# Cross-attention on one core: row tiles weighed two at a time, and the output projection of 14 batches in products of fp16 parts

## The chip, the cores and the metric

One core of a Trainium2 chip runs the whole program. The metric is the device time of one execution in microseconds (us), as the median over several runs of the same kernel. TensorE does the matrix products (the profile shows its products as PE and its weight loads as PEld), VectorE is DVE, ScalarE is ACT, GpSimd is POOL, SyncE is SP. SP computes nothing here: it issues nearly all DMA transfers, and its row in the trace is the time that it spends on issuing them.

## The reference, cut to what matters

For each of B = 16 batches there are 100 query rows (`x`) and 1444 context rows (`ctx`), all 128 wide; there are H = 16 heads of width 64.

```python
q = (x @ Wq + bq).reshape(b, 100, 16, 64)
k = (ctx @ Wk + bk).reshape(b, 1444, 16, 64)
v = (ctx @ Wv + bv).reshape(b, 1444, 16, 64)
attn = softmax(einsum('bqhd,bkhd->bhqk', q, k) / 8)
out = einsum('bhqk,bkhd->bqhd', attn, v).reshape(b, 100, 1024) @ Wo + bo
z = x + out
result = (z - mean(z)) * rsqrt(var(z) + 1e-5) * gamma + beta
```

## The kernel before, in words

**The algebra.** The kernel never forms keys or values. For each head it folds the key weights into the query (`a_sb`, 128x128 a head) and the value weights into the output weights (`m_sb`, 128x128 a head, in 32-bit floats). For a batch it projects the queries (`project_queries`, L390, and from batch 3 on `project_queries_16`, L396, of fp16 parts), scores them against the context itself, weighs the context itself with the softmax, and projects the weighed context out with `m_sb` (`project_out`, L403).

**Row tiles.** The 16 x 100 = 1600 (head, query) rows of a batch are cut in tiles of 128. A batch fills 12.5 tiles, so two batches share 25: tiles 0 to 11 of the even batch, tile 12 (the mixed tile) half of each, tiles 13 to 24 of the odd batch. There are N = 200 tiles in all.

**Precision.** Every large operand is split in two fp16 parts, hi and lo. The scores of a tile are three products (hi x hi, hi x lo, lo x hi) over three stretches of 482, 482 and 480 keys, nine instructions (L537). The weighing of a tile (`weigh`, L540) takes the softmax transposed, with the keys in 12 blocks of 128: for 11 blocks `pt_hi` against `c_hi` and `c_lo` (22 products of 128 columns, L551), then 12 products with `pt_lo` (L556). The weights are the context block, the moving operand is the softmax tile. All 34 add up in 128 columns of one PSUM bank (`O_BANK`), in the mixed tile twice 34 products of 64 columns.

**One tile through the engines.** PE scores tile n into one of two sets of three banks (L537). DVE takes the row maximum (L757). ACT takes the exponential and the row sum (L871); DVE takes the reciprocal (L763, L765); ACT writes the hi part `p_hi` (L879), and DVE the lo part `p_lo` (L772). SP transposes both by DMA (`transpose_hi`, L331, issue at L336; `transpose_lo`, L338, issue at L344) into `pt_hi` and `pt_lo`, rings of PTS = 3 tiles; each transpose waits until the tile that had its place is weighed. PE weighs tile n in its iteration n + LAG, LAG = 4. ACT copies the result out of `O_BANK` into `o_t`, scaled back (`take_result`, L889), and only then may PE start the next weighing.

**The loop of PE** (L609) is, for each n: scores of tile n, weighing of tile n - 4, and a job. The order is written out by hand, and every engine works through its own list in that order. `window(n)` (L89) gives the batch w whose tiles are scored and the place r in it, 0 to 12. The jobs are set by r: the queries of batch w + 1 in four groups of four heads at r = 1 to 4 (moved by DVE at L700, split by POOL in `split_queries`, L958); the output projection of batch w - 1 in four groups of four heads at r = 6 to 9 (`FIN_AT`, L582 to L595), a 128x128 32-bit product a head with the 100 `o_t` columns as weights; the spreading of a maximum at r = 10 (L455). At r = 9 DVE adds the residual and takes mean and variance (`take_rows`, L781), and POOL finishes the rows (`inverse_deviation`, L991, and `scale_rows`, L998). DVE also takes the maximum of the context of batch w + 2 at r = 6 to 8, ACT makes `c_hi` at r = 4, 6 and 7 (L853), POOL makes `c_lo` (L975). SP loads context at r = 1 to 3 and stores a result at r = 2. After the last tile come four weighings with parts of the last output projection between them (L623 to L630), and the rows of the last batch.

**PSUM.** Banks 0 to 5 are the scores, 6 is `O_BANK`, 7 is `JOB_BANK`.

## Time and profile before

| | |
|---|---|
| Median of 3 runs | 902.93 us (902.35 to 903.62) |
| The profiled execution: its own time | 902.63 us |
| Its span, first to last instruction | 900.7 us |
| Mean granted TensorE clock | 0.989 |
| Busy: PE, PEld, DVE, ACT, POOL | 880.5, 678.1, 812.7, 752.2, 335.9 us |
| Moved by DMA | 181.17 MB, mean 201 GB/s |

The profile shows one execution. Products are pipelined, so one of them is shown longer than the distance at which they follow each other; the distance is read from how long a run of them takes in the chain of waits. "DMA share" is the time that packets took as a share of the 16 engines' time; packets overlap, so it can be above 1. "SPq" is SP's queue.

### The profile page before, as it was taken

The page shows a single profiled execution, that of the slowest core. Times are in us where ns is not written, and L with a number is a line of the kernel's source. Part 1 is how long each engine was busy: PE and PEld are TensorE (multiplying, and loading weights), DVE is VectorE, ACT ScalarE, POOL GpSimd, SP SyncE. Part 2 cuts the span into 40 slices and gives each one's busy share as a digit, 9 for nine tenths or more (in the row PEclk, how much of TensorE's full clock was granted, in tenths as well). Part 3 has the DMA queues.
Part 4 walks back from the last instruction along what each step waited for, and adds up shares of the span by engine and source line. Part 5 has one row for each costly group of instructions (what it writes and reads, how often), then busy time and mean ns, then how long its engine had stood idle before and what let it go on. Part 6 is the DMA issues. An engine that isn't in the chain of part 4 may idle for free.

```text
span 900.7 us, 25456 instructions
## 1 busy us (share of the span) xinstructions
PE 880.5 (98%) x10366; PEld 678.1 (75%) x10366; DVE 812.7 (90%) x1042; ACT 752.2 (84%) x1081; POOL 335.9 (37%) x385
## 2 busy tenths in 40 slices
PE   8799989999999999999999999999999999999997
PEld 7476877777777777777777777777777777777776
DVE  4899879999999999989999999999999999998983
ACT  3687878888888888888889888888888889888983
POOL 3042596534415253342424434152442525144011
PEclk8899999999999999999999999999999999999999
DMA  8598998999999999999999999999999999999996
GB/s 235 130 181 176 187 192 165 211 209 201 222 206 207 215 200 215 199 211 221 206 216 210 209 211 218 214 205 212 206 224 199 207 221 196 205 204 204 204 172 121
DMA packets 683065, 181.17 MB, mean 201 GB/s; under 512 B 654596, under 2 KB 682052, under 8 KB 682948
## 3 DMA queue, kind: packets, MB, share of 16 engines
q1 hardware_dynamic: 681332, 178.48, 105.1%
q8 instruction: 82, 1.34, 0.7%
q10 hardware_dynamic: 1344, 0.53, 0.2%
q0 software_dynamic: 272, 0.53, 0.2%
q14 instruction: 35, 0.29, 0.1%
HBM read 15.35 MB, written 0.82 MB: 18 GB/s over the span
## 4 chain that ended last, share of the span: by engine, by line
PE 89%; DVE 4%; POOL 3%; ACT 2%; issue 1%; DMA 1%; POOLq 0%; SPq 0%; DVEq 0%; ACTq 0%
PE ps L537 38%; PE ps L551 26%; PE ps L556 14%; PE ps L405 6%; PE ps L399 3%; DVE nmax L757 1%; DVE p_lo L772 1%; PE ps L392 1%; ACT p L871 1%; POOL early_sb L1017 1%; PE ps L458 1%; POOL c_lo L986 1%; DMA o_t<-in_L_xattn_Wq_dram 1%; POOL x_sb L1048 1%; POOL c_scaled L1015 0%
## 5 line engine op out<-in xcount | busy, mean ns | idle before, releaser
L772 DVE SCALAR_TENSOR_TENSOR p_lo<-p,rinv,p_hi 128x1444 f16<-128x1444 f32 x200 | 347.5, 1738 | 6.5 <-ACT p_hi L879 6.1
L879 ACT ACTIVATE p_hi<-p,rinv 128x1444 f16<-128x1444 f32 x200 | 299.8, 1499 | 49.3 <-DVE rinv L765 33.9
L757 DVE TENSOR_REDUCE nmax<-ps 128x1 f32<-128x1446 f32 x200 | 329.8, 1649 | 7.4 <-PE ps L537 7.4
L871 ACT ACTIVATE p<-ps,nmax 128x1446 f32<-128x1446 f32 x200 | 292.0, 1460 | 13.2 <-DVE nmax L757 12.9
L551 PE MATMUL ps<-pt_hi,c_hi 128*128 128x128 f16 (+1 forms) x2288 | 269.2, 217 | 0.7 <-ACT o_t L894 0.7
L551 PE MATMUL ps<-pt_hi,c_lo 128*128 128x128 f16 (+1 forms) x2288 | 269.1, 217 | 0.0
L551 PEld LDWEIGHTS ps<-pt_hi,c_hi 128*128 128x128 f16 x2288 | 217.5, 98 | 24.8 <-issue 3.4
L551 PEld LDWEIGHTS ps<-pt_hi,c_lo 128*128 128x128 f16 x2288 | 217.3, 98 | 20.3 <-issue 0.3
L537 PE MATMUL ps<-ct_hi,g_hi 128*128 128x482 f16 (+3 forms) x624 | 156.8, 370 | 1.6 <-DVE ps L727 0.9
L556 PE MATMUL ps<-pt_lo,c_hi 128*128 128x128 f16 (+1 forms) x2288 | 157.0, 217 | 0.0
L537 PE MATMUL ps<-ct_hi,g_lo 128*128 128x482 f16 (+3 forms) x624 | 156.2, 368 | 0.0
L537 PE MATMUL ps<-ct_lo,g_hi 128*128 128x482 f16 (+3 forms) x624 | 155.8, 367 | 0.0
L963 POOL CAST g_hi<-g_raw 128x400 f16<-128x400 f32 x60 | 31.0, 517 | 304.3 <-DVE g_raw L700 304.3
L556 PEld LDWEIGHTS ps<-pt_lo,c_hi 128*128 128x128 f16 x2288 | 132.2, 98 | 0.0
L894 ACT ACTIVATE o_t<-ps,unscale 128x128 f32<-128x128 f32 (+1 forms) x208 | 73.9, 359 | 65.2 <-PE ps L556 64.3
L986 POOL TENSOR_TENSOR c_lo<-c_scaled,c_hi 128x512 f16<-128x512 f32 x45 | 87.0, 1932 | 77.3 <-ACT c_hi L853 73.3
L537 PEld LDWEIGHTS ps<-ct_hi,g_lo 128*128 128x128 f16 (+1 forms) x624 | 59.0, 99 | 64.9 <-issue 1.5
L537 PEld LDWEIGHTS ps<-ct_lo,g_hi 128*128 128x128 f16 (+1 forms) x624 | 59.0, 99 | 64.9 <-issue 1.5
L537 PEld LDWEIGHTS ps<-ct_hi,g_hi 128*128 128x128 f16 (+1 forms) x624 | 53.6, 100 | 25.8 <-issue 2.6
L886 ACT ACTIVATE p_lo<-p,rinv 128x72 f16<-128x72 f32 x200 | 69.9, 349 | 0.0
L405 PE MATMUL ps<-m_sb,o_t 128*100 128x128 f32 x512 | 68.7, 277 | 0.2 <-ACT o_t L894 0.2
L763 DVE TENSOR_SCALAR rsum<-psums 128x1 f32<-128x1 f32 x200 | 30.6, 153 | 35.3 <-ACT p L871 26.4
(108 smaller groups left out, 728.0 us busy)
## 6 DMA issues: line engine op xcount, KB each, us to landing
c_raw<-in_ctx_dram SPq DMA_DIRECT2D x32, 256.0 KB
pt_hi<-p_hi SPq DMA_TRANSPOSE x200, 3.5
pt_lo<-p_lo SPq DMA_TRANSPOSE x200, 3.9
c_raw<-in_ctx_dram SPq DMA_DIRECT2D x16, 192.0 KB
c_raw<-in_ctx_dram SPq DMA_DIRECT2D x48, 18.0 KB
out_dram<-late_sb SPq DMA_DIRECT2D x16, 50.0 KB
x_sb<-in_x_dram SPq DMA_DIRECT2D x1, 600.0 KB
o_t<-in_L_xattn_Wq_dram SPq DMA_DIRECT2D x2, 256.0 KB, 4.3
```

What stands on the lines that cost most here:

```text
L405: mm = pe.matmul(bank[0:QL, 0:P], o_t[:, par, h * QL:(h + 1) * QL], m_sb[:, h, :], start=(h == 0), stop=(h == H - 1), skip_group_check=True)
L537: mm = pe.matmul(ps[at:at + rows, bank + k, 0:e - a], g, ct, start=(part == 0), stop=(part == 2))
L551: pe.matmul(out_t, c[:, b % 2, t, :], pt_hi[:, n % PTS, t, at:at + rows], start=(t == 0 and c is c_hi), stop=False)
L556: mm = pe.matmul(out_t, c, pt_lo[:, n % PTS, t, at:at + rows], start=False, stop=(t == KT - 1))
L757: dve.tensor_reduce(nmax[:, n % RING:n % RING + 1], ps[:, bank:bank + 3, 0:KEYW], AX.XY, ALU.max, negate=True).then_inc(s_nm, 1)
L772: dve.scalar_tensor_tensor(out=p_lo[:, n % LOS, 0:KL], in0=p32[:, n % P32S, 0:KL], scalar=rinv[:, i:i + 1], in1=p_hi[:, par, 0:KL], op0=AL ...
L871: act.activation(p32[:, n % P32S, :].rearrange("p (k w) -> p k w", w=KEYW), ps[:, bank:bank + 3, 0:KEYW], ACT.Exp, bias=nmax[:, i:i + 1], ...
L879: act.activation(p_hi[:, par, 0:KL], p32[:, n % P32S, 0:KL], ACT.Copy, scale=rinv[:, i:i + 1]).then_inc(s_hi, 1)
L886: act.activation(p_lo[:, n % LOS, KL:KL + 2 * KTAIL].rearrange("p (i k) -> p i k", i=2), tail, ACT.Copy, scale=rinv[:, i:i + 1]).then_inc( ...
L894: act.activation(o_t[:, b % 2, row:row + rows], ps[:, O_BANK, at:at + rows], ACT.Copy, scale=unscale[:, b % UNSCALES:b % UNSCALES + 1]).th ...
L963: pool.tensor_copy(g_hi[:, par, cols], query_group(g)).then_inc(s_part, 1)
L986: pool.tensor_tensor(c_lo[:, par, tiles, :].rearrange("p t d -> p (t d)"), c_scaled[:, :], c_hi[:, par, tiles, :].rearrange("p t d -> p (t ...
```

## The change

Row tiles are joined in units: tiles (0,1), (2,3) to (10,11), the mixed tile alone, (13,14) to (23,24), 13 units in a pair of batches. `pt_hi` and `pt_lo` now hold three units. A unit of two is weighed by the same 34 weights, each with a moving operand of 2 x 128 columns, into 256 columns of the bank. In the iteration that is 4 after the unit's first tile PE does the products of the first nine hi blocks (18 products), in the next one the other two hi blocks and the lo blocks (4 + 12 products). The mixed tile is weighed as before. ACT takes a unit's result in one instruction of 256 columns, in the second of these iterations. After the last tile the last unit is weighed in two parts between parts of the last output projection.

For batches 1 to 14 the output projection takes three fp16 products a head (hi x hi, lo x hi, hi x lo). `m16`, the parts of `m_sb`, is made once: maxima by DVE at n = 17 to 20, the spread and the scale at n = 22, hi by ACT at n = 23 to 26, lo by POOL in window 2. `o16`, the parts of `o_t`, is made by POOL for each of the 14 batches, group by group, in front of `split_queries` of the same group, and the last group after the fourth. The scaling back moves from ACT's copy to DVE's residual addition, with a factor that POOL makes (`output_scale`). The rows of the last batch are finished by DVE instead of POOL. `m16` and `o16` lie in the memory of `a_sb` and `xT`.

Core of the diff (semaphores, small tiles and blank lines left out):

```diff
-    assert HALF == P // 2
+    assert HALF == P // 2 and WHOLE % 2 == 0
     IN_PAIR = 2 * WHOLE + 1
     MIXED = WHOLE
-    SEGS = WHOLE + 1
+    UNITS = WHOLE + 1
+    RESULTS = WHOLE // 2 + 1
...
+    FIRST_TILES = 9
...
+    def unit(n):
         pair, i = divmod(n, IN_PAIR)
-        return 2 * SEGS * pair + i + (1 if i > MIXED else 0)
+        u, place = divmod(i, 2) if i < MIXED else (MIXED // 2, 0) if i == MIXED else divmod(i + 1, 2)
+        return UNITS * pair + u, place
+    def tiles_of(u):
+        pair, j = divmod(u, UNITS)
+        first = IN_PAIR * pair + 2 * j - (1 if j > MIXED // 2 else 0)
+        return (first,) if j == MIXED // 2 else (first, first + 1)
+    def results_of(u):
+        tiles = tiles_of(u)
+        if len(tiles) == 1:
+            return segments(tiles[0])
+        b, row, rows, at = segments(tiles[0])[0]
+        return ((b, row, 2 * P, 0),)
...
+    def in_parts(b):
+        return 0 < b < B - 1
...
-        pt_hi = sb("pt_hi", [P, PTS, KT - 1, P], F16)
-        pt_lo = sb("pt_lo", [P, PTS, KT, P], F16)
+        pt_hi = sb("pt_hi", [P, PTS, 2, KT - 1, P], F16)
+        pt_lo = sb("pt_lo", [P, PTS, 2, KT, P], F16)
...
+        m16 = a_sb[:, :, :].rearrange("p h e -> p (h e)").bitcast(F16).rearrange("p (h i e) -> p h i e", i=2, e=P)
+        o16 = xT[:, :, :].rearrange("p b q -> p (b q)").bitcast(F16).rearrange("p (i r) -> p i r", i=2)
...
+        MPARTS_AT = 17
+        MTOP_AT = IN_PAIR // 2 + TOP_AT
+        M16_AT = MTOP_AT + 1
...
             def transpose_hi(n):
                 par = n % 2
                 sp.wait_ge(s_hi, n + 1)
-                if n >= PTS:
-                    sp.wait_ge(s_pv, segments_before(n - PTS + 1))
-                sp.dma_start_transpose(pt_hi[:, n % PTS, :, :], p_hi[:, par, 0:(KT - 1) * P]).then_inc(s_th[par], 16)
+                u, place = unit(n)
+                if u >= PTS:
+                    sp.wait_ge(s_pv, results_before(u - PTS + 1))
+                sp.dma_start_transpose(pt_hi[:, u % PTS, place, :, :], p_hi[:, par, 0:(KT - 1) * P]).then_inc(s_th[par], 16)
...
+            def project_out_16(bank, heads):
+                for h in heads:
+                    rows = slice(QL * h, QL * (h + 1))
+                    for i, j in ((0, 0), (1, 0), (0, 1)):
+                        mm = pe.matmul(bank[0:QL, 0:D], o16[:, i, rows], m16[:, h, j, :], start=(h == 0 and i == j),
+                                       stop=(h == H - 1 and j == 1))
                 return mm
...
-            def weigh(n):
-                par = n % 2
-                for i, (b, row, rows, at) in enumerate(segments(n)):
-                    out_t = ps[:, O_BANK, at:at + rows]
-                    if n > 0:
-                        pe.wait_ge(s_ot, segments_before(n))
+            def weigh_hi(u, tiles, first):
+                if first and u > 0:
+                    pe.wait_ge(s_ot, results_before(u))
+                for n in tiles_of(u):
+                    pe.wait_ge(s_th[n % 2], halves(n))
+                for b, row, rows, at in results_of(u):
+                    if first and tiles_of(u)[0] == first_tile(b):
+                        pe.wait_ge(s_chl, b + 1)
+                    weigh_part(u, b, rows, at, [(c, pt_hi, t) for t in tiles for c in (c_hi, c_lo)], first, False)
+            def weigh_lo(u):
+                for n in tiles_of(u):
+                    pe.wait_ge(s_tl[n % LOS], turns(n))
+                for b, row, rows, at in results_of(u):
+                    weigh_part(u, b, rows, at, [(c_hi, pt_lo, t) for t in range(KT - 1)] + [(c_tail, pt_lo, KT - 1)],
+                               False, True).then_inc(s_pv, 1)
+            def weigh_mixed(u):
+                n, = tiles_of(u)
+                pe.wait_ge(s_ot, results_before(u))
+                for b, row, rows, at in results_of(u):
                     if n == first_tile(b):
                         pe.wait_ge(s_chl, b + 1)
-                    pe.wait_ge(s_th[par], halves(n))
-                    for t in range(KT - 1):
-                        for c in (c_hi, c_lo):
-                            pe.matmul(out_t, c[:, b % 2, t, :], pt_hi[:, n % PTS, t, at:at + rows],
-                                      start=(t == 0 and c is c_hi), stop=False)
+                    pe.wait_ge(s_th[n % 2], halves(n))
+                    weigh_part(u, b, rows, at, [(c, pt_hi, t) for t in range(KT - 1) for c in (c_hi, c_lo)], True, False)
                     pe.wait_ge(s_tl[n % LOS], turns(n))
-                    for t in range(KT):
-                        c = c_hi[:, b % 2, t, :] if t < KT - 1 else c_tail[:, b % 2, :]
-                        mm = pe.matmul(out_t, c, pt_lo[:, n % PTS, t, at:at + rows], start=False, stop=(t == KT - 1))
-                    mm.then_inc(s_pv, 1)
+                    weigh_part(u, b, rows, at, [(c_hi, pt_lo, t) for t in range(KT - 1)] + [(c_tail, pt_lo, KT - 1)],
+                               False, True).then_inc(s_pv, 1)
+            def weigh_part(u, b, rows, at, products, first, last):
+                out_t = ps[:, O_BANK, at:at + rows]
+                for i, (c, pt, t) in enumerate(products):
+                    weights = c_tail[:, b % 2, :] if c is c_tail else c[:, b % 2, t, :]
+                    moving = pt[:, u % PTS, 0, t, at:at + rows] if rows < P else pt[:, u % PTS, :, t, :]
+                    mm = pe.matmul(out_t if rows < P else split(out_t, 2, P), weights, moving, start=(first and i == 0),
+                                   stop=(last and i == len(products) - 1))
+                return mm
+            def weigh(n):
+                if 0 <= n - LAG < N:
+                    u, place = unit(n - LAG)
+                    if len(tiles_of(u)) == 1:
+                        weigh_mixed(u)
+                    elif place == 0:
+                        weigh_hi(u, range(FIRST_TILES), True)
+                if 0 <= n - LAG - 1 < N:
+                    u, place = unit(n - LAG - 1)
+                    if len(tiles_of(u)) == 2 and place == 0:
+                        weigh_hi(u, range(FIRST_TILES, KT - 1), False)
+                        weigh_lo(u)
...
-                        pe.wait_ge(s_ot, SEGS * w)
-                    mm = project_out(bank, (w - 1) % 2, range(HG * g, HG * (g + 1)))
+                        if w == 1:
+                            pe.wait_ge(s_ot, RESULTS * w)
+                        else:
+                            pe.wait_ge(s_ml, NG)
+                    if in_parts(w - 1):
+                        pe.wait_ge(s_os, NG * (w - 2) + g + 1)
+                        mm = project_out_16(bank, range(HG * g, HG * (g + 1)))
+                    else:
+                        mm = project_out(bank, (w - 1) % 2, range(HG * g, HG * (g + 1)))
...
+                    if n == MTOP_AT:
+                        pe.wait_ge(s_mc, 1)
+                        pe.matmul(bank[:, P:2 * P], spread(m_max[:, :]), ident[:, :], start=True, stop=True).then_inc(s_mt, 1)
...
+            last = unit(N - 1)[0]
+            pe.wait_ge(s_z, B - 1)
+            done = project_last(0, last - 1)
+            weigh_hi(last, range(KT - 1), True)
+            done = project_last(done, last)
+            weigh_lo(last)
+            pe.wait_ge(s_ot, 2 * RESULTS * (B // 2))
+            project_out(ps[:, JOB_BANK, :], (B - 1) % 2, range(done, H)).then_inc(s_fin, 1)
...
+        def finish_rows(eng, b):
+            par = b % 2
+            eng.wait_ge(s_rd, b + 1)
+            eng.tensor_scalar(zn[:, par, :], z[:, par, :], mv[:, par, 0:1], rstd[:, par:par + 1], ALU.subtract,
+                              ALU.mult).then_inc(s_zn, 1)
+            eng.wait_ge(s_zn, b + 1)
+            eng.tensor_tensor(zg[:, par, :], zn[:, par, :], rows_b[0:QL, 1, :], ALU.mult).then_inc(s_zg, 1)
+            eng.wait_ge(s_zg, b + 1)
+            if b > 1:
+                eng.wait_ge(s_out[par], 16 * (b // 2))
+            eng.tensor_tensor(y[:, par, :], zg[:, par, :], rows_b[0:QL, 2, :], ALU.add).then_inc(s_y, 1)
...
+                if in_parts(b):
+                    dve.wait_ge(s_fu, b)
+                    dve.scalar_tensor_tensor(out=z[:, par, :], in0=ps[0:QL, JOB_BANK, 0:D], scalar=fin_un[0:QL, par:par + 1],
+                                             in1=x_sb[:, b, :], op0=ALU.mult, op1=ALU.add).then_inc(s_z, 1)
+                else:
+                    dve.tensor_tensor(z[:, par, :], ps[0:QL, JOB_BANK, 0:D], x_sb[:, b, :], ALU.add).then_inc(s_z, 1)
...
             take_rows(B - 1)
+            finish_rows(dve, B - 1)
...
-            def take_result(n):
-                for i, (b, row, rows, at) in enumerate(segments(n)):
-                    act.wait_ge(s_pv, segments_before(n) + len(segments(n)))
+            def take_result(u):
+                for i, (b, row, rows, at) in enumerate(results_of(u)):
+                    act.wait_ge(s_pv, results_before(u) + len(results_of(u)))
                     if row == 0 and b > 1:
                         act.wait_ge(s_fin, b - 1)
                     act.activation(o_t[:, b % 2, row:row + rows], ps[:, O_BANK, at:at + rows], ACT.Copy,
-                                   scale=unscale[:, b % UNSCALES:b % UNSCALES + 1]).then_inc(s_ot, 1)
+                                   scale=O_PART if in_parts(b) else unscale[:, b % UNSCALES:b % UNSCALES + 1]).then_inc(s_ot, 1)
+            def take_results(n):
+                if n - LAG < N and len(tiles_of(unit(n - LAG)[0])) == 1:
+                    take_result(unit(n - LAG)[0])
+                if n > LAG and unit(n - LAG - 1)[1] == 0 and len(tiles_of(unit(n - LAG - 1)[0])) == 2:
+                    take_result(unit(n - LAG - 1)[0])
...
+                if M16_AT <= n < M16_AT + NG:
+                    g = n - M16_AT
+                    act.wait_ge(s_ms, 1)
+                    if g == 0:
+                        act.wait_ge(s_16, NG)
+                    act.activation(m16[:, HG * g:HG * g + HG, 0, :], m_sb[:, HG * g:HG * g + HG, :], ACT.Copy,
+                                   scale=m_scale[:, :]).then_inc(s_mh, 1)
...
+            def split_results(b, g):
+                pool.wait_ge(s_ot, results_taken(b, HG * QL * (g + 1)))
+                if g == 0 and b > 1:
+                    pool.wait_ge(s_fin, b)
+                cols = query_columns(g)
+                pool.tensor_copy(o16[:, 0, cols], o_t[:, b % 2, cols]).then_inc(s_oh, 1)
+                pool.wait_ge(s_oh, NG * (b - 1) + g + 1)
+                pool.tensor_tensor(o16[:, 1, cols], o_t[:, b % 2, cols], o16[:, 0, cols], ALU.subtract).then_inc(s_os, 1)
+            def output_scale(b):
+                pool.wait_ge(s_mu, 1)
+                if b > 2:
+                    pool.wait_ge(s_z, b - 1)
+                pool.tensor_scalar(fin_un[:, b % 2:b % 2 + 1], unscale[:, b % UNSCALES:b % UNSCALES + 1], m_un[:, :], 1.0 / O_PART,
+                                   ALU.mult, ALU.mult).then_inc(s_fu, 1)
+            def leave_m_lo(g):
+                heads, at = slice(HG * g, HG * g + HG), c_scaled[:, :].rearrange("p (n w) -> p n w", w=P)
+                pool.wait_ge(s_mh, g + 1)
+                if g:
+                    pool.wait_ge(s_ml, g)
+                pool.tensor_scalar(at, m_sb[:, heads, :], m_scale[:, :], 1.0, ALU.mult, ALU.mult).then_inc(s_mw, 1)
+                pool.wait_ge(s_mw, g + 1)
+                pool.tensor_tensor(m16[:, heads, 1, :], at, m16[:, heads, 0, :], ALU.subtract).then_inc(s_ml, 1)
...
+                        if w == 2:
+                            leave_m_lo(g)
+                        if g < NG - 1 and in_parts(w - 1):
+                            split_results(w - 1, g)
                         split_queries(b, g)
+                    if w == 2:
+                        pool.wait_ge(s_ml, NG)
+                if in_parts(w - 1):
+                    if b == B:
+                        for g in range(NG - 1):
+                            split_results(w - 1, g)
+                    split_results(w - 1, NG - 1)
+                    output_scale(w - 1)
+                if b < B:
...
-                    scale_rows(w - 1)
+                    finish_rows(pool, w - 1)
             inverse_deviation(B - 1)
-            scale_rows(B - 1)
```

## Rows read from the trace of the kernel before

**Rows 1.** Stretches: a pair of batches, then a plain, a query and a projection tile.

```profile
core 0: us, PE busy (x) PEld busy (x) DVE busy (x) ACT busy (x) POOL busy (x), PEclk, DMA share, GB/s
406.30:512.17 105.87, 105.87 (x1285) 81.46 (x1286) 100.24 (x127) 92.38 (x133) 39.71 (x46) 1.00 1.15 214
457.52:461.26 3.74, 3.74 (x45) 2.77 (x43) 3.71 (x5) 3.52 (x5) 0.00 (x0) 1.00 1.21 256
473.55:477.83 4.28, 4.28 (x57) 3.31 (x55) 4.25 (x7) 3.67 (x5) 1.62 (x3) 1.00 0.93 222
490.49:495.13 4.64, 4.64 (x52) 3.67 (x51) 4.61 (x6) 4.16 (x7) 0.67 (x1) 1.00 1.12 175
```

**Rows 2.** Chain of waits, start us, us, what: PE's kinds of work.

```profile
92.50 0.92 PE ps L392 x8
...
418.28 0.54 PE ps L399 x12
...
431.19 1.84 PE ps L537 x9
433.03 1.23 PE ps L551 x22
434.26 0.67 PE ps L556 x12
434.93 0.91 PE ps L405 x8
```

**Rows 3.** Groups of instructions, shapes apart: count, busy us, mean ns, idle before.

```profile
L551 PEld LDWEIGHTS ps<-pt_hi,c_hi 128*128 128x128 f16 x2288 | 217.5, 98 | 24.8 <-issue 3.4 <-ACT o_t L894 1.3
L537 PEld LDWEIGHTS ps<-ct_hi,g_lo 128*64 128x64 f16 x48 | 2.7, 110 | 2.2
L405 PEld LDWEIGHTS ps<-m_sb,o_t 128*100 128x100 f32 x512 | 58.3, 167 | 0.4 <-ACT o_t L894 0.4
L963 POOL CAST g_hi<-g_raw 128x400 f16<-128x400 f32 x60 | 31.0, 517 | 304.3 <-DVE g_raw L700 304.3
L965 POOL TENSOR_TENSOR g_lo<-g_raw,g_hi 128x400 f16<-128x400 f32 x60 | 56.8, 947 | 4.9
L853 ACT ACTIVATE c_hi<-c_raw,alpha 128x512 f16<-128x512 f32 x48 | 33.7, 707 | 0.3 <-DVE alpha L694 0.3
```

**Rows 4.** Order of time on ACT, over one plain tile: start us, us, instruction.

```profile
843.23 1.50 ACT L879 ACTIVATE p_hi<-p,rinv 128x1444 f16<-128x1444 f32 x1 [0.17 <-DVE rinv L765]
844.74 0.37 ACT L894 ACTIVATE o_t<-ps,unscale 128x128 f32<-128x128 f32 x1
845.00 1.46 ACT L871 ACTIVATE p<-ps,nmax 128x1446 f32<-128x1446 f32 x1
...
846.97 1.50 ACT L879 ACTIVATE p_hi<-p,rinv 128x1444 f16<-128x1444 f32 x1 [0.18 <-DVE rinv L765]
```

**Rows 5.** SP's queue: issues of tile 91, then of tile 109 (hi parts).

```profile
434.91 1.42 SPq L336 DMA_TRANSPOSE pt_hi<-p_hi  x1
...
509.55 1.53 SPq L336 DMA_TRANSPOSE pt_hi<-p_hi  x1
```

**Rows 6.** The tile pt_hi: from issue to landing.

```profile
DMA to landing us min/median/max: 3.1/3.5/6.0
```

**Rows 7.** Chain of waits again: the weighings that started in iterations 94 and 112.

```profile
437.68 1.23 PE ps L551 x22
...
514.13 1.33 PE ps L551 x22
```

**Rows 8.** Order of time: the rows of the last batch.

```profile
894.95 0.29 DVE L787 TENSOR_TENSOR late_sb<-ps,x_sb 100x128 f32<-100x128 f32 x1 [7.36 <-PE ps L405]
...
896.87 0.81 POOL L1001 TENSOR_SCALAR late_sb<-late_sb,mv,rstd 100x128 f32<-100x128 f32 x1
897.76 0.46 POOL L1004 TENSOR_TENSOR late_sb<-late_sb,rows_b 100x128 f32<-100x128 f32 x1
898.29 0.45 POOL L1008 TENSOR_TENSOR late_sb<-late_sb,rows_b 100x128 f32<-100x128 f32 x1
```

97 lines of the change are left out of this document (65 added, 32 removed).

## The prediction

> **What bounds the kernel now.** I read the stretches first. In a pair of batches PE works 105.87 of 105.87 us at a granted clock of 1.00; DVE works 100.24, ACT 92.38, POOL 39.71 [rows 1]. So PE has no gap at all in the steady part, and each us taken from its list is a us of the run until the next engine is met. That is DVE, 5.6 us a pair below. The chain of waits says the same: it stays on PE, from line to line without a wait, from about 135 us to 874 us, and [rows 2] is what it passes. Nine score products take 1.84 us. The 34 weighing products take 1.23 + 0.67 = 1.90 us. That is a plain tile, 3.74 us. Four heads of queries add 0.54 us, four heads of output projection 0.91 us (4.28 and 4.64 us [rows 1]).
>
> The distance between products shows what a product costs. 34 products of 128 columns in 1.90 us are 55.8 ns each; 128 columns at 2.4 GHz, the clock granted there, are 53.3 ns. The query products of 100 columns stand 0.54 / 12 = 45 ns apart, against 41.7 of streaming, the scores 204 ns apart against 200.8 for 482 columns [rows 2]. So streaming sets the distance, with 2.5 to 3.6 ns on top of each product. The weight load of 98 ns [rows 3] is no limit: it is longer than the distance of 55.8 and still delays nothing.
>
> **Weighing by two.** A unit of two tiles had 68 products of 128 columns, 2 x 1.90 = 3.79 us. It gets 34 of 256 columns. The columns are the same, half of the fixed parts go. With 106.7 ns of streaming and 2.5 to 3.6 ns on top, the unit takes 3.71 to 3.75 us and 44 to 82 ns are saved. I take 3.0 ns: 65 ns, and for 96 units **6.2 us** (4.2 to 7.9). Halving the number of weight loads gives nothing more, since they were covered.
>
> **The output projection.** 16 heads in four groups of 0.905 us (4.645 - 3.74 [rows 1]) are 3.62 us a batch. After: 48 fp16 products with 128 moving columns. The nearest row is the weighing's, 55.8 ns, so 2.68 us. Saved: 0.94 us a batch, in 14 batches **13.2 us**. The doubt is in the weights: `o16` is 100 columns wide, and no row has an fp16 load of 100 columns. The rows around it: 98 ns for 128 fp16 columns, but 110 ns for 64, so narrower loads are not quicker; 167 ns for 100 columns of 32 bits, which stand at 0.91 / 8 = 113 ns [rows 2, 3]. There the reported load is longer than the distance too, so part of it is always latency. Where a load does bind is the 32-bit query projection, 128 weight columns against 100 moving ones: 0.92 / 8 = 115 ns [rows 2], more than the 83 ns of its two passes of streaming; that is 0.9 ns a column of 32 bits. Half the bytes make 0.45 ns a column, some 45 ns for 100, covered by 55.8. The dear end is the 113 ns at which the 32-bit load of the same shape passes: 48 of them are 5.4 us, 1.8 us more than now, +25 us in 14 batches. The cheap end is 45 ns, the query product's distance: 2.14 us, 20.7 us saved. I take 55.8.
>
> The Trainium skill (TensorE: Matmul & The Clock Gate, Weight-path perf modes) says that the fast weight load applies only with 128 weights of a type other than FP32, and (LDWEIGHTS) that a plain load takes its columns over 1.2 GHz. By that an `o16` load is an estimated 83 ns, the projection 4.0 us a batch and the change here a loss of 5 us instead of a gain of 13. The row of 110 ns for 64 columns against 98 ns for 128 agrees that the narrow load is the slower kind; how long it holds PE no row shows.
>
> **What is added beside PE.** POOL splits the results: for each group a cast and a subtraction as for the queries, 0.52 + 0.95 = 1.46 us [rows 3], so 5.9 us a batch, 12 us a pair on 39.71 of 106. POOL's queue is in order, so what stands behind matters: `split_queries`, `context_lo`, the rows. Groups 0 to 2 wait for results that were taken in an earlier window; the last waits for the batch's last result, at r = 3 or 4, and is done at about r = 5, while PE asks for it at r = 9. `context_lo` waits for `c_hi` at r = 4, 6 and 7 anyway, and POOL was idle 304 us in front of its casts alone [rows 3]. I take nothing; without this cover it would cost its 5.9 us a batch. DVE's added instruction replaces one of its kind.
>
> Once only: `m16` costs DVE four maxima, ACT 4 x 0.71 us (the `c_hi` copy, of this shape) [rows 3] at n = 23 to 26, where tiles are shortest, POOL four groups in window 2, PE one product (0.3 us). ACT falls behind by up to 2 us there. I take 0.3 for PE and 0.7 us for late transposes after it; POOL's part (some 22 us from n = 26) ends just before PE asks for it at n = 31.
>
> **ACT's copy.** 208 copies become 112, wider. From a unit's first to its second iteration ACT saves one. A plain tile's loop through ACT and DVE is hi part to hi part 3.74 us, in which the copy takes 0.27 (844.73 to 845.00) [rows 4]. Without a copy it is 3.47, with a wide one, growing with the columns, about 3.85: 3.66 on average. PE's plain tile will be 3.71. This loop stays below PE, narrowly.
>
> **The wait that the change moves.** A unit's first products need the hi transposes of both tiles. The second tile's has to be there three iterations after its scores, not four. In tile 109, a second tile, the issue was at 509.55 us, landing 3.5 us later at 513.05, and iteration 112's weighing started at 514.13: 1.1 us to spare [rows 5 to 7]. In tile 91, also a second tile, it was issued at 434.91, landed at 438.41, and iteration 94's weighing began at 437.68: 0.7 us too late. I went through 92 of the 96 second tiles this way: four would be late, by 0.1 to 0.9 us, and eleven more have less than 1 us to spare, most of them behind the context loads (r = 3 to 5) or at r = 9 to 12. Two things shift that: PE's three tiles get shorter by 0.2 to 0.6 us, which takes; and the ring of three units frees the transposes from waiting for the weighing just before, which held back those of query and projection tiles by 0.5 to 0.9 us, and gives. I take **1.5 us** of stalls over the run (0 to 12). What waits behind PE then is only PE's own list.
>
> **The end.** DVE finishes the last rows instead of POOL: 0.81 + 0.46 + 0.45 us become three DVE instructions of about 0.29 [rows 8]: 0.85 us less. The last unit's result comes in one piece, which leaves three heads to project behind it where two stood: 0.25 us more. Net **0.6**.
>
> **Sum.** 900.7 - 6.2 - 13.2 - 0.6 + 0.3 + 0.7 + 1.5 = 883.2 us of span. The profiled execution took 902.63, so 1.9 us lie outside the span, and it stood 0.3 us below the median: 883.2 + 1.9 + 0.3 = 885.4, said as **885 us**. A pair of batches would take 105.87 - 12 x 0.065 - 8 x 0.235 = 103.2 us, above DVE's 100.2.
>
> **The rivals.**
> *Late transposes.* The odd hi parts keep missing the shorter deadline. For: SP issues nearly without a pause, and tile 91. Against: the margin of tile 109, and the freed ring. If two second tiles a window come 0.4 us late, 16 windows give 12.8 us in place of 1.5: 896 us.
> *The loop of ACT and DVE.* DVE's busy time is 97% of the new 103.2, and it works 4.25 of 4.28 us in a query tile [rows 1]. If waits between the engines hold a pair at 104.5, eight pairs give back 10 us: 895 us. Against: it needs losses that today's gapless PE doesn't show.
> *Loads of `o16` in the open (slower).* If a 100-column fp16 load holds PE for as long a column as the 32-bit one (0.9 ns), a product takes 90 ns, a batch 4.3 us, and 14 batches lose 10 us instead of gaining 13.2: 885.4 + 23 = 908 us. It decides from the distance of products: the other parts bring some 4 us, so above 3.62 + 4 / 14 = 3.9 us a batch, 81 ns a product, the change loses. For: the 110 ns of the narrow load. Against: half the bytes.
> *No gain from pairs.* If 256 columns in two strides cost 8 ns on top, weighing is where it was: 891 us.
>
> **How the numbers follow.** Forecast 0.62, late transposes 0.13, the loop 0.08, loads 0.08, no gain from pairs 0.09. The forecast's own range is 881 to 889. Against 902.93, 0.2% is 1.8 us, about what a measurement can tell from no change. All cases but the loads, and the far end of late transposes, are faster: 0.90; the same 0.04; slower 0.06. The range reaches down to 880 (2.5 ns on top and no stalls) and up to 897, which takes in the late transposes and leaves the loads out.
>
> **What would show it.** A pair of batches of 103.2 us; weighing products 109.7 ns apart and the unit at 3.73 us; four heads of fp16 projection in 0.67 us; PE without gaps in front of `weigh_hi`. Wrong if PE stands before a unit's first product on a transpose, if the twelve products of a group take over 0.9 us, or if PE's idle time grows to more than 3 us between 140 and 870 us.

## The result and the profile after

| | before | after |
|---|---|---|
| Median | 903.27 us (902.35 to 904.58, 4 runs) | 890.23 us (888.62 to 891.75, 4 runs) |
| Ratio | | 0.9849, 95% interval 0.9827 to 0.9870 |
| Profiled execution: own time, span | 902.63, 900.7 us | 888.62, 886.8 us |
| A pair of batches (tiles 75 to 99) | 105.87 us | 102.85 us |

The change makes the kernel 13.0 us faster. The forecast was 885 us, 5.2 us below what was measured. Of the executions of the experiments below one, of the run e11, took 1117.92 us at a mean granted clock of 0.749; no comparison uses it, and the other five of e11 have a median of 889.47 us. First the page's busy line of the kernel after, then two of its stretches, one of them a pair of batches without a stall, to set beside [rows 1]; the columns are those of the header.

```profile
PE 860.3 (97%) x7328; PEld 618.4 (70%) x7328; DVE 832.9 (94%) x1053; ACT 732.0 (83%) x989; POOL 483.2 (54%) x516
```

```profile
core 0: us, PE busy (x) PEld busy (x) DVE busy (x) ACT busy (x) POOL busy (x), PEclk, DMA share, GB/s
353.78:456.63 102.85, 102.85 (x908) 73.87 (x906) 101.05 (x127) 89.50 (x121) 60.59 (x64) 1.00 1.10 218
...
456.00:560.00 104.00, 102.87 (x907) 73.71 (x905) 101.42 (x124) 89.26 (x120) 60.00 (x64) 1.00 1.10 212
```

In the first stretch PE has no gap and DVE is 1.8 us below it. In the second PE idles 1.13 us. DVE is busier over the run than before (832.9 us against 812.7), although the change gives it little new to do (four maxima of 0.68 us and the last rows). The products, in the chain of waits (start us, us, what), against [rows 2]:

```profile
227.86 2.13 PE ps L642 x18
229.98 0.67 PE ps L458 x12
...
290.27 1.75 PE ps L642 x16
292.02 0.67 PE ps L458 x12
294.53 1.97 PE ps L642 x18
```

A unit's 16 + 18 products take 1.75 + 1.97 = 3.72 us, 109.4 ns a product; 18 products take 2.13 where they begin behind a stall. Four heads of the fp16 projection take 0.67 us, 56 ns a product, against 0.91 us. The costly groups of the kernel after (count, busy us, mean ns, idle before):

```profile
L921 DVE SCALAR_TENSOR_TENSOR p_lo<-p,rinv,p_hi 128x1444 f16<-128x1444 f32 x200 | 367.9, 1840 | 2.4 <-ACT p_hi L1038 2.0
...
L1147 POOL CAST xT<-o_t 128x400 f16<-128x400 f32 x56 | 88.9, 1588 | 13.1 <-ACT o_t L1053 13.1
L1149 POOL TENSOR_TENSOR xT<-o_t,xT 128x400 f16<-128x400 f32 x56 | 53.0, 947 | 4.6
...
L458 PEld LDWEIGHTS ps<-a_sb,xT 128*100 128x100 f16 x672 | 44.3, 125 | 2.3 <-issue 1.7
```

`p_lo` (L921, before L772 with a mean of 1738 ns) has grown by 102 ns, 20.4 us over 200 tiles: as much as DVE's whole 20 us. The cast of the results (L1147, into `o16`, which lies in `xT`) takes 1588 ns where the cast of the same shape took 517 [rows 3]. These two numbers are one thing. In order of time, DVE and POOL of the kernel after:

```profile
207.12 1.66 DVE L906 TENSOR_REDUCE nmax<-ps 128x1 f32<-128x1446 f32 x1
207.26 0.52 POOL L1137 CAST g_hi<-g_raw 128x400 f16<-128x400 f32 x1 [9.61 <-DVE g_raw L831]
207.86 0.95 POOL L1139 TENSOR_TENSOR g_lo<-g_raw,g_hi 128x400 f16<-128x400 f32 x1
208.69 1.71 DVE L921 SCALAR_TENSOR_TENSOR p_lo<-p,rinv,p_hi 128x1444 f16<-128x1444 f32 x1
208.75 2.02 POOL L1147 CAST xT<-o_t 128x400 f16<-128x400 f32 x1
210.86 0.95 POOL L1149 TENSOR_TENSOR xT<-o_t,xT 128x400 f16<-128x400 f32 x1
...
212.35 0.94 POOL L1139 TENSOR_TENSOR g_lo<-g_raw,g_hi 128x400 f16<-128x400 f32 x1
212.81 1.99 DVE L921 SCALAR_TENSOR_TENSOR p_lo<-p,rinv,p_hi 128x1444 f16<-128x1444 f32 x1
213.24 1.95 POOL L1147 CAST xT<-o_t 128x400 f16<-128x400 f32 x1
```

At 208.75 POOL's cast starts just behind `p_lo` and ends 2.02 us later, 0.37 us after `p_lo`: the cast waits for `p_lo`. At 212.81 `p_lo` starts while POOL is in a subtraction and takes 1.99 us in place of 1.71: `p_lo` waits for POOL. Sorted by what POOL was doing, the 67 `p_lo` with POOL idle average 1.72 us, the 12 that met mostly L1149 2.15, the 15 that met mostly L1139 2.02. The row maximum (L906), which reads PSUM, is 1.65 us beside any of them. What decides is how much of POOL's subtraction is left when `p_lo` starts: with 0.12 us left `p_lo` takes 1.71, with 0.48 left 1.99, with 0.57 left 2.08, with 0.64 left 2.15, so that what is added is 0.2 us less than what was left. The Trainium skill (SBUF — State Buffer, SBUF: two separate sides) states this: VectorE with two SBUF inputs and a GpSimd instruction that reads SBUF share a port pair by an exclusive lock, and the later one is blocked for the whole instruction of the earlier. The trace agrees for POOL's 128-row casts and subtractions, down to which of DVE's instructions is touched (`p_lo` has two inputs in SBUF). It does not fit POOL's scaling of 100 rows (L774): 14 `p_lo` start with 0.40 to 0.46 us of it left and take 1.71.

Where PE then stood. I measured the distance from tile to tile: the six pairs from tile 25 to 174 take 107.75, 103.36, 102.86, 104.15, 103.92 and 103.04 us. Six pairs without a stall would be 617.2, so 7.9 us are lost, 4.9 of them in the first. From 200 to 860 us PE waits only for transposes (us, times, the longest):

```profile
PE ps L642 <- DMA pt_hi<-p_hi: 3.3, 5, 1.1
```

Two of these waits, of 0.90 and 1.13 us, are of this kind (SP's queue, then the chain, then ACT in order of time, of the kernel after):

```profile
218.04 2.79 SPq L393 DMA_TRANSPOSE pt_hi<-p_hi  x1
220.89 0.58 SPq L348 DMA_DIRECT2D c_raw<-in_ctx_dram  x1
221.53 1.30 SPq L352 DMA_DIRECT2D c_raw<-in_ctx_dram  x3
222.94 1.30 SPq L402 DMA_TRANSPOSE pt_lo<-p_lo  x1
224.35 1.41 SPq L393 DMA_TRANSPOSE pt_hi<-p_hi  x1
```

```profile
223.65 0.70 ACT p_hi L1038
224.35 3.38 DMA pt_hi<-p_hi
227.72 0.14 issue
227.86 2.13 PE ps L642 x18
```

```profile
219.52 1.50 ACT L1038 ACTIVATE p_hi<-p,rinv 128x1444 f16<-128x1444 f32 x1 [0.46 <-DVE rinv L914]
```

The transpose of a second tile (41) stands behind a slow one, a context load and the three tail loads of r = 3; it is issued at 224.35, lands at 227.72, and PE, which had stood since 226.96, starts. The chain names ACT's `p_hi` of 223.65 as the releaser, and that is misleading: it is the `p_hi` of the next tile. That of tile 41 is the one of 219.52 and was over at 221.02, so the transpose stood 3.3 us in SP's queue with its input ready. The wait of 0.89 us (PE at 596.74) is of another kind: there the transpose stood 1.1 us in the queue and took 5.5 us to land, against a median of 3.5. The first pair has another stall, in order of time:

```profile
171.18 2.10 POOL L1163 TENSOR_SCALAR c_scaled<-m_sb,m_scale 128x512 f32<-128x512 f32 x1
...
173.37 1.16 POOL L1165 TENSOR_TENSOR a_sb<-c_scaled,a_sb 128x512 f16<-128x512 f32 x1
...
174.62 0.84 PE L458 MATMUL ps<-a_sb,xT 128*100 128x128 f16 x12 [1.44 <-issue]
```

PE waits 1.44 us for POOL's last lo part of m, and starts 0.1 us after it ended.

### The profile page after: what moved, and what is told of

The parts are those of the page before. It is cut to its first block, busy times and chain, and to the rows that moved or that the text cites. A ratio compares the mean times of both kernels' runs of the same rounds, so it can differ in the third digit from the quotient of the medians.

```text
span 886.8 us, 19588 instructions
## 1 busy us (share of the span) xinstructions
PE 860.3 (97%) x7328; PEld 618.4 (70%) x7328; DVE 832.9 (94%) x1053; ACT 732.0 (83%) x989; POOL 483.2 (54%) x516
## 4 chain that ended last, share of the span: by engine, by line
DVE 43%; PE 38%; issue 8%; ACT 5%; DMA 5%; SPq 2%; ACTq 0%; DVEq 0%; POOLq 0%; POOL 0%
DVE p_lo L921 20%; PE ps L642 17%; DVE nmax L906 16%; PE ps L603 16%; DMA pt_hi<-p_hi 4%; ACT p L1030 2%; PE ps L458 2%; ACT p_hi L1038 2%; DVE rsum L912 2%; PE ps L450 1%; DVE rinv L914 1%; DVE c_max L808 1%; PE ps L465 1%; DMA bq_pairs<-in_L_xattn_bq_dram 1%; SPq L402 1%
## 5 line engine op out<-in xcount | busy, mean ns | idle before, releaser
L921 DVE SCALAR_TENSOR_TENSOR p_lo<-p,rinv,p_hi 128x1444 f16<-128x1444 f32 x200 | 367.9, 1840 | 2.4 <-ACT p_hi L1038 2.0
L906 DVE TENSOR_REDUCE nmax<-ps 128x1 f32<-128x1446 f32 x200 | 330.0, 1650 | 6.0 <-PE ps L603 6.0
L642 PE MATMUL ps<-pt_hi,c_hi 128*128 128x256 f16 (+1 forms) x1232 | 253.6, 261 | 5.4 <-DMA pt_hi<-p_hi 3.8
L642 PE MATMUL ps<-pt_hi,c_lo 128*128 128x256 f16 (+1 forms) x1232 | 253.4, 261 | 0.0
L642 PEld LDWEIGHTS ps<-pt_hi,c_hi 128*128 128x128 f16 x1232 | 114.4, 98 | 43.0 <-issue 10.4
L642 PE MATMUL ps<-pt_lo,c_hi 128*128 128x256 f16 (+1 forms) x1232 | 138.7, 261 | 0.0
L642 PEld LDWEIGHTS ps<-pt_hi,c_lo 128*128 128x128 f16 x1232 | 113.8, 98 | 29.5 <-issue 0.5
L642 PEld LDWEIGHTS ps<-pt_lo,c_hi 128*128 128x128 f16 x1232 | 109.6, 98 | 11.9
L1186 POOL TENSOR_TENSOR c_lo<-c_scaled,c_hi 128x512 f16<-128x512 f32 x45 | 98.3, 2184 | 24.7 <-ACT c_hi L1012 22.1
L1147 POOL CAST xT<-o_t 128x400 f16<-128x400 f32 x56 | 88.9, 1588 | 13.1 <-ACT o_t L1053 13.1
L1139 POOL TENSOR_TENSOR g_lo<-g_raw,g_hi 128x400 f16<-128x400 f32 x60 | 58.0, 967 | 4.8
```

What stands on the lines that cost most here:

```text
L642: mm = pe.matmul(out_t if rows < P else split(out_t, 2, P), weights, moving, start=(first and i == 0), stop=(last and i == len(products) - 1))
L906: dve.tensor_reduce(nmax[:, n % RING:n % RING + 1], ps[:, bank:bank + 3, 0:KEYW], AX.XY, ALU.max, negate=True).then_inc(s_nm, 1)
L921: dve.scalar_tensor_tensor(out=p_lo[:, n % LOS, 0:KL], in0=p32[:, n % P32S, 0:KL], scalar=rinv[:, i:i + 1], in1=p_hi[:, par, 0:KL], op0=AL ...
L1139: pool.tensor_tensor(g_lo[:, par, cols], query_group(g), g_hi[:, par, cols], ALU.subtract).then_inc(s_gs, 1)
L1147: pool.tensor_copy(o16[:, 0, cols], o_t[:, b % 2, cols]).then_inc(s_oh, 1)
L1186: pool.tensor_tensor(c_lo[:, par, tiles, :].rearrange("p t d -> p (t d)"), c_scaled[:, :], c_hi[:, par, tiles, :].rearrange("p t d -> p (t ...
```

## The experiments

The theory: PE's list got shorter by about what was worked out, and the loss is stalls of PE, from transposes that came late because DVE and ACT were held up through the port shared with POOL. The rival: the second tile's shorter deadline alone. "Lost" below is the time of tiles 25 to 174 over six pairs without a stall (102.86 us each, 104.48 without the fp16 projection; e9, e11 and e12 have 0.8 us of one 32-bit projection in it). It and `p_lo` come from one profiled execution each, the medians from 4 to 12 executions; for e2 there is no pair without a wait to compare with. The two do not always agree: the profiled execution was the fastest of the four in the changed kernel (888.62) and the slowest of the four in e7 (894.25) and e10 (887.57), and in the profiled executions tile 25 starts anywhere from 141.9 to 145.9 us.

| run | median us | ratio (95%) | lost | `p_lo` ns |
|---|---|---|---|---|
| the changed kernel | 890.23 | 0.9849 (0.9827 to 0.9870) | 7.9 | 1840 |
| e1 pairs alone | 895.83 | 0.9905 (0.9887 to 0.9923) | 0.5 | 1751 |
| e2 parts alone | 898.21 | 0.9931 (0.9915 to 0.9948) | - | 1834 |
| e3 no splits | 885.12 | 0.9789 (0.9770 to 0.9809) | 4.3 | 1761 |
| e4 no lo part of m | 887.33 | 0.9807 (0.9784 to 0.9829) | 5.2 | 1830 |
| e5 before, with splits | 903.82 | 0.9995 (0.9983 to 1.0006) | 0 | 1775 |
| e6 LAG 5 | 891.76 | 0.9868 (0.9853 to 0.9884) | 8.0 | 1829 |
| e7 casts twice | 891.21 | 0.9864 (0.9845 to 0.9882) | 11.5 | 1790 |
| e8 LAG 5, no splits | 887.37 | 0.9814 (0.9799 to 0.9829) | 2.4 | 1749 |
| e9 m later | 889.80 | 0.9840 (0.9821 to 0.9859) | 7.2 | 1834 |
| e10 loads spread | 885.49 | 0.9793 (0.9774 to 0.9812) | 4.8 | 1831 |
| e11 all three | 889.78 | 0.9840 (0.9824 to 0.9856) | 6.9 | 1823 |
| e12 e9 with e10 | 886.41 | 0.9813 (0.9789 to 0.9836) | 5.6 | 1825 |

The ratios are to the kernel before in the same comparison.

**e1, the pairs alone.**

```diff
     def in_parts(b):
-        return 0 < b < B - 1
+        return False
```
(and the instructions that make `m16` and its scale are left out)

> The units of two tiles alone, the output projection in 32 bits as before, nothing added on POOL. In the changed kernel a unit's products stand 109.2 ns apart, so 96 units save 8 us, and the last rows on DVE about 0.6. Theory of the port (POOL's added casts and subtractions stretch DVE's p_lo, DVE falls behind, the hi transposes come late and PE stands): without the added POOL work there are no stalls, 894.5 us, p_lo 1.74 us as before. Rival, the shorter deadline of the second tile (three iterations in place of four): it is here as it was, so the stalls stay and 3 to 7 us of the gain are lost: 897 to 901 us.

895.83 us, 0.9905. Pairs of batches of 104.48 to 104.53 us but for one of 104.93. Between 200 and 860 us PE waited on nothing but this:

```profile
PE ps L642 <- DMA pt_hi<-p_hi: 0.4, 1, 0.4
```

With PE's list at 104.48 us a pair, 1.6 us longer than in the changed kernel, the deadline alone costs 0.4 us. The rival falls in this form; e3 has the deadline together with the short list.

**e2, the parts alone.**

```diff
     def tiles_of(u):
-        pair, j = divmod(u, UNITS)
...
+        return (u,)
```
(a unit is one tile; weighing, copies and the weighings at the end as in the kernel before, the last rows stay on DVE)

> The fp16 output projection alone, tiles weighed one at a time, each with four iterations for its transposes. PE's list gets 14 x 0.94 = 13.2 us shorter and POOL's added work is all there. Theory of the port: p_lo rises to some 1.82 us, some 5 us are lost around the splitting of m and little after: 894 to 896 us. Rival, the shorter deadline: it is not here, so there are no stalls and the 13.2 us come in full, with 0.6 from the end: 889.5 us.

898.21 us, a gain of 0.69% where by the prediction's working the list got 13.2 us shorter: 7 us lost, without any shorter deadline, and 2 us more than the theory said. Windows 2 and 3 take 108.3 us, the later pairs 104.35 to 105.2, and PE waits for `o_t`, ACT's copy, which it never did before:

```profile
PE ps L632 <- ACT o_t L1036: 1.8, 6, 0.3
```

The two halves add up: 0.9905 x 0.9931 = 0.9837, within the interval of both together.

**e3, POOL's splits left out.**

```diff
-                pool.tensor_copy(o16[:, 0, cols], o_t[:, b % 2, cols]).then_inc(s_oh, 1)
...
-                pool.tensor_tensor(o16[:, 1, cols], o_t[:, b % 2, cols], o16[:, 0, cols], ALU.subtract).then_inc(s_os, 1)
+                pool.tensor_copy(o16[0:1, 0, cols.start:cols.start + 1], o_t[0:1, b % 2, cols.start:cols.start + 1]).then_inc(s_os, 1)
```
(`o16` is a tile of its own that stays zero but for single elements: the kernel leaves the 14 projections out of its result, while PE does the same products)

> The changed kernel with POOL's splitting of the results left out (o16 is a tile of its own and stays zero but for single elements, so the projection adds nothing; PE's products are the same). Left: the splitting of m in window 2. Theory of the port: p_lo falls from 1.84 to about 1.77 us, DVE gains some 13 us of slack, the stalls of the steady part go (2 to 4 us) and window 2 loses less: 885 to 887 us. Rival, the shorter deadline: within 1 us of the changed kernel, 890.

885.12 us, as the theory had it, with `p_lo` back at 1761 ns:

```profile
L921 DVE SCALAR_TENSOR_TENSOR p_lo<-p,rinv,p_hi 128x1444 f16<-128x1444 f32 x200 | 352.1, 1761 | 2.5 <-ACT p_hi L1038 2.2
```

But 2.2 of the 3.0 us of stalls in the last five pairs stayed. The gain that the trace shows is in windows 2 and 3 (104.98 against 107.75 us). So the splits of the results are not what makes most of the late transposes. How little they add can be read on the way of a second tile from the start of its scores: over the second tiles from 50 to 174, `p_hi` is ready after 7.70 us here, 7.69 in e1 and 7.98 in the changed kernel; then it stands 0.8 to 0.9 us in SP's queue (1.7 to 1.9 for the tiles at r = 4 and 5, behind the loads) and lands 3.7 to 3.9 us later, at worst 5.5 to 5.7. The port adds 0.3 us to a way of 12.7.

**e4, no lo part of m** (two instructions a group shrunk to one element; m's lo part is zero in the products).

> The changed kernel with POOL's lo parts of m left out (eight POOL instructions of window 2, each 0.7 to 2.2 us, become tiny ones; m's lo part is zero, PE's products are the same). In the changed kernel's trace window 2 takes 4 us more than the windows of the same place after it. Theory of the port: most of it goes, 886.5 us. Rival, that ACT's four copies of m or the jitter of the DMAs made it: 889 to 890 us.

887.33 us, nearer to the theory's 886.5 than to the rival's 889 to 890. Windows 2 and 3 take 105.57 us, and the tile of 6.79 us in which PE had waited for POOL takes 4.47.

**e5, the splits added to the kernel before** (the added code of `split_results`, PE waiting for it).

> The kernel before with POOL's casts and subtractions of the results added (into a tile that nobody reads; PE waits for them as in the changed kernel, the projection stays in 32 bits). Nothing is taken off PE. Theory of the port: p_lo goes from 1.74 to some 1.82 us and DVE from 100.2 to about 102 us a pair of batches, but PE's list is 105.9 us a pair and every tile has four iterations, so it is covered: 903 to 905 us. Rival, that POOL's work costs its own time wherever it stands, as in the run of the parts alone, which gave up 7 us of 13: 909 to 911 us.

903.82 us, 0.9995: no difference. `p_lo` rose to 1775 ns, and every pair from tile 25 on is 105.87 or 105.88 us. The same splits on POOL whose absence gives 5 us in the changed kernel (e3) cost nothing where PE's list is longer by 3 us a pair. They also lengthen `p_lo` less here: by 37 ns, against 79 ns between e3 and the changed kernel.

**e6, LAG 5.**

```diff
-    LAG = 4
+    LAG = 5
-    CHI_AT = (4, 6, 7)
+    CHI_AT = (5, 6, 7)
```

> The changed kernel with LAG 5 in place of 4 (and the first copy of c_hi one place later, at r = 5): a unit's second tile has four iterations for its transposes again, as every tile had before. POOL's work stays. If the late transposes are what PE stands for (8 us over the run, 5 of them in windows 2 and 3), they go and some 1 us comes on at the end: 883 to 885 us. If DVE itself were the bound (97% busy), a longer lag would bring nothing: 889 to 891 us.

891.76 us: missed, by 7. Two costs hid the gain. From the start of the last scores to the end it is 25.1 us against 22.0, since a whole unit more is weighed behind the scores (34 + 22 + 12 products stand there in one chain). And windows 2 and 3 rose to 109.1 us: PE waits 2.13 us for POOL, since no lag helps against that, and behind this wait the granted clock fell to 0.50, the lower of its two levels (1.2 GHz, against 2.4), in this profiled execution:

```profile
176.00:179.00 3.00, 3.00 (x9) 1.07 (x8) 1.96 (x4) 2.82 (x4) 2.92 (x3) 0.50 0.65 140
```

Nine score products took 3.47 us there in place of 1.84, so some 1.8 us of what e6 lost is the clock. No wait for a transpose is left in PE's list, but six for ACT's copy, 1.9 us.

**e7, each cast twice.**

```diff
-                pool.tensor_copy(o16[:, 0, cols], o_t[:, b % 2, cols]).then_inc(s_oh, 1)
+                for i in range(2):
+                    pool.tensor_copy(o16[:, 0, cols], o_t[:, b % 2, cols]).then_inc(s_oh, 1)
```
(with the wait in the loop)

> The changed kernel with each of POOL's 56 casts of results done twice. Theory of the port: p_lo rises again, by half of what the splits added (1.84 to 1.88 us, some 8 us of DVE), DVE passes PE's 102.9 us a pair in places: 893 to 896 us. Rival, the deadline alone: 890 to 891 us.

891.21 us: missed. `p_lo` fell to 1790 ns instead of rising. A second cast moved which of POOL's instructions `p_lo` meets: 27 `p_lo` start within a subtraction of the results, with 0.22 us of it left on average, and take 1.78 us, where in the changed kernel 14 do with 0.64 left and take 2.16. What counts is not how much POOL works but how much of an instruction is left when `p_lo` starts. The steady pairs are as in the changed kernel; windows 2 and 3 take 112.3 us. The first of two long tiles there (9.93 us) has a wait of 3.75 us for POOL, the second (6.37) has none: behind the wait the granted clock fell to 0.50.

```profile
180.00:185.00 5.00, 5.00 (x23) 2.62 (x22) 0.22 (x1) 0.93 (x2) 4.69 (x7) 0.50 1.23 188
```

Neither in the changed kernel nor in any other run of this list did the clock fall between tiles 25 and 174.

**e8, LAG 5 without the splits.**

> LAG 5, with the splitting of the results left out on POOL (the projection adds nothing, PE's products are the same). It parts the two causes: if a longer lag already takes the stalls away, this is within 1 us of LAG 5 with the splits, 883 to 885 us; if the port costs by itself, it is 3 us or more below that.

887.37 us, again with the 25.1 us at the end. Here the steady part is clean: after windows 2 and 3 all five pairs take 102.86 or 102.87 us, where e3 (LAG 4) had 102.86 to 104.10 and e6 (with splits) 102.88 to 103.56. So each of the two has its share: the lag takes away the waits for transposes, the splits cost some 0.4 us a pair at LAG 5, where ACT's copy is what PE waits for (at LAG 4 the traces differ by 0.2 a pair, less than single executions do), and in windows 2 and 3 2.8 us at LAG 4 and 3.9 at LAG 5, of which the clock is 1.8.

**e9, m later.**

```diff
-        return 0 < b < B - 1
+        return 1 < b < B - 1
...
                     context_lo(b)
+                    if w == 2:
+                        for g in range(NG):
+                            leave_m_lo(g)
```

> The changed kernel, but m's lo parts are made by POOL behind the context of batch 3 (end of window 2) and the fp16 projection starts with batch 2 in place of 1: 13 batches, so PE gets 0.94 us more. In the changed kernel's trace windows 2 and 3 take 107.75 us against 102.9 for a pair without stalls; 2.3 us of it is PE in front of the first group of the projection (6.79 us for a tile of 4.47), where POOL had only just ended its last lo part. If POOL's chain in window 2 is what costs there, that pair comes to about 104.5 with the 0.94 in it: 887.5 us. If it were the jitter of the start, nothing is gained and 0.9 lost: 891 us.

889.80 us. The pair of windows 2 and 3 went from 107.75 to 106.33 with the 0.8 us of the 32-bit batch in it, but not to 104.5: the second tile behind the loads came late there as it did in the changed kernel (tile 44, 5.74 us, and 5.54 there, in place of 4.47). Not to be told from the changed kernel.

**e10, the loads spread.**

```diff
-    LOAD_AT = 1
-    STORE_AT = 2
+    LOAD_AT = 0
+    STORE_AT = 5
```
(and the three tail loads one place behind the last large one; window 0 still starts at 1)

> The changed kernel with SP's context loads at r = 0, 1, 2, the three small tail loads at r = 3 and the store at r = 5, in place of loads at 1, 2, 3 with the tails behind the last and the store at 2. The late second tiles of the steady part stand behind that burst (places 8 and 19 of a pair). If the burst makes them late, most of the 3 us of stalls in the last five pairs go: 887.5 us. If it only moves the burst onto the tiles before, 890.

885.49 us, the fastest that computes everything, 4.7 us below the changed kernel, more than the 3 expected. By the ratios it is 5.1 us, with an interval of 2.5 to 7.7. The traces show 3.1 of them: 4.8 us lost in place of 7.9. The last five pairs take 102.97, 102.93 and three times 102.86 us. PE's waits from 200 us to 860 us are none, with `p_lo` as long as ever:

```profile
L923 DVE SCALAR_TENSOR_TENSOR p_lo<-p,rinv,p_hi 128x1444 f16<-128x1444 f32 x200 | 366.2, 1831 | 1.9 <-ACT p_hi L1040 1.6
```

```profile
353.78:456.63 102.85, 102.83 (x908) 73.83 (x906) 101.00 (x127) 89.40 (x121) 60.56 (x64) 1.00 1.12 218
```

The tiles at r = 4 and 5 stand 1.2 us in SP's queue on average, in place of 1.7, and none more than 2.8 us. The edit moves the large loads, the tails and the store; no run parts them.

**e11, three edits** (LAG 5 for units that start before tile 190 and 4 from there, m later, loads spread).

> Three edits together: LAG 5 for all units but those of the last window's end (from tile 190 on 4 again, since LAG 5 paid 3.1 us behind the last scores: 25.1 us from the start of the last scores to the end against 22.0), m's lo parts later with 13 batches in fp16, and the spread loads. Pairs of 102.9 us throughout with LAG 5 if POOL's splits cost 0.5 us a pair as they did there, 22.5 us behind the last scores: 885 to 886 us, the fastest of all that compute everything. If LAG 5 loses elsewhere what it gains, 888 to 890.

889.78 us: missed. The end is 22.0 us again, but the stretch from tile 175 to the last scores takes 99.2 us against 97.0, with one tile of 6.96 us (194), the one in which the lag changes: most of what the end had cost is paid there. And the last five pairs are 103.3 to 104.0 us: PE waits for ACT's copy nine times, 3.1 us in all from 140 to 860 us, most often at r = 1, where tiles take 4.4 and 4.76 us in place of 4.34.

**e12, e9 with e10.**

> The spread loads (885.5 us) and m's lo parts later with 13 batches in fp16 (889.8 us), with LAG 4. The second alone brought 1.4 us in windows 2 and 3 and had a late second tile of 1.3 us in them; with the burst of loads gone that stall should go too: that pair from 107.5 to about 105 us, the others 102.86. 883 us. If the two overlap, 885 to 886.

886.41 us: not to be told from e10. Windows 2 and 3 did come to 105.5 us, but in this profiled execution the pair of tiles 150 to 174 took 105.35 us for late transposes: the last five pairs lost 2.9 us, as in the changed kernel. So spread loads do not rule late transposes out, and that e10's trace has none may be in part the luck of one execution. The medians are the stronger evidence: 885.49 against 890.23, and with m later 886.41 against 889.80. No version found is faster than e10.

## Why the prediction came out as it did

**Right: PE's list.** The pair was put at 103.2 us and is 102.85. The weighing's fixed part is 2.7 ns a product in place of 3.0; the fp16 projection is 0.67 us for four heads to the digit. From tile 25 to 174 the list is 18 us shorter (six times 3.02), the working had 16. These distances explain only part of the difference: by them a unit saves 75 ns, but in e1 a pair is 1.39 us shorter, 116 ns for each of its 12 units, and where the other 41 ns come from no run shows.

**Right: the loads of `o16`.** The rival of uncovered loads is out: 125 ns are reported for a load of 100 fp16 columns, and the products with them stand 56 ns apart. The estimate of 83 ns after the Trainium skill's plain load (TensorE: Matmul & The Clock Gate, LDWEIGHTS) is contradicted by this row: a load holds PE for no more than 56. "No gain from pairs" is out too.

**Wrong: "I take nothing" for POOL's splitting.** The step counted POOL's time and its queue, and found both covered. It did not ask what POOL's instructions do to DVE. All that POOL got to do added 20.4 us to `p_lo`, and 15.8 of them go with the splits of the results (1840 to 1761 ns in e3). DVE had 5.6 us a pair to give, by the stretch rows, and the change's gain had used 3 of them already. e3 puts the splits at 5 us of the run by the medians (2.8 us of it are seen in windows 2 and 3, 0.9 in the later pairs), e5 at nothing when PE's list is the long one. The price of a helper engine was in the trace before: `p_lo` had a mean of 1738 ns and was 1.72 us when POOL was idle.

**Wrong: POOL's part of m "ends just before PE asks for it".** It was put at 22 us from n = 26 with casts of 0.52 and subtractions of 0.95; with half of them held to 2 us by `p_lo` it took 27.7 us, of which POOL was idle 3.9, and came 1.4 us too late. All stalls of windows 2 and 3 together are 4.9 us where 1.0 stood. e4 takes away 2.2 of them, e3 2.8.

**Wrong in size: late transposes.** 1.5 us were taken; 3.0 are there in the last five of the six pairs. The mechanism and the places were right: the tiles for which PE waits from 200 us on stand at r = 4 and 5, behind the context loads, and at r = 9 and 12. Tile 91 was in time here; it came late in e3 and e9. What it takes is the short deadline and PE's short list together, with a burst or a slow transpose in SP's queue: e1 has the deadline with the longer list and loses 0.4, e3 has deadline and short list without the splits and loses 2.2, e8 has the short list without the deadline and loses nothing in those pairs, e10 has deadline, list and port and only the loads moved, and loses 0.2 (e12, with the loads moved too, 2.9). The freed ring did not outweigh it.

**The end** was put at 0.6 us less and is 22.0 against 22.5.

The sum of span: 883.2 forecast, 886.8 measured. Between tiles 25 and 174 some 2.1 us more came off PE's list than was worked out, and 5.7 us more were lost in stalls (7.9, where 1.5 and 0.7 stood). That the first makes up for a third of the second is luck. 890.23 lies outside the forecast's own range of 881 to 889; the range up to 897 has it, because it took the late transposes in. The median lies 1.6 us above the profiled execution, which was the fastest of the four; 0.3 had been allowed. The rival of late transposes (896) had a part in it, not at its price; the one of the ACT and DVE loop (895) is not borne out as it was put, since a pair of 102.85 us does occur with DVE busy for 101.05 of it.

**The signs.** Two of the three signs of being wrong came: PE stood on a transpose before a unit's first products, and its idle time between 140 and 870 us is 6.8 us, more than the 3 that were named. The third did not: twelve products take 0.67 us.

**Open** is what makes the executions of one kernel differ (888.6 to 891.8 us in the changed kernel). Slow transposes are a candidate: of the 400 issues in SP's queue 9 to 48 take 2.3 us or more in every trace, against a median of 1.4, and no run here chose when. Open is also where the rest of e3's and e10's gain lies, 5 us by the medians and 3.6 and 3.1 in the time lost between tiles 25 and 174.

## What to carry to other kernels

When work moves off the engine that has no gaps, put a price on the engine that gets it and on each engine that shares something with it: read one instruction of the second-busiest engine beside an idle and beside a busy neighbour. A gain ends where the second engine begins, and near that point small bursts on a queue decide; moving loads and a store by one to three places brought back some 5 us by the medians, 3 of them seen in the traces. A profile's releaser is inferred: before blaming the engine that it names, check that it is that tile's own instruction. A longer pipeline is paid at its end, so look at the time behind the last input before trusting the steady part.

## What the runs showed of the hardware that was not expected

POOL's cast of 128 x 400 took 0.52 us beside DVE's reduction out of PSUM and 1.5 to 2.0 us beside `p_lo`; `p_lo` took 0.43 us longer when it started with 0.64 us of one of POOL's 400-column subtractions left, and not longer when 0.12 us were left. Doubling the casts shortened `p_lo` (1790 against 1840 ns). A 100-column fp16 weight load is reported with 125 ns and a 128-column one with 98, and both pass at 56 ns a product. Behind PE's wait for POOL in tile 31 the granted clock fell to its lower level where the wait was 2.13 and 3.75 us (e6, e7), and not where it was 1.44 and 1.60 (the changed kernel, e2).
